# A transformer kernel whose first stage projects values in fp32 and keys as three products of rounded and remaining parts

## The reference, cut to what matters

```
x = x + matmul(fake_quant(layernorm(x)), fake_quant(ctx))            # layer 0 "attention", per batch
x = x + mx_linear(silu(mx_linear(n, w_gate)) * mx_linear(n, w_up), w_down)     # n = layernorm(x)
    # mx_linear quantises its input to 6 bits and its weight to 4 bits, with one exponent per 32 values
k = ctx @ wk    # 8 key heads of 128, 2 batches of 512 context rows
v = ctx @ wv    # 8 value heads of 128
x = x + softmax(rope(q) rope(k)^T / sqrt(128)) v @ wo                # 32 query heads
x = x + (silu(n @ gate) * (n @ up)) @ down                           # layer 1, ternary weights
```

## Time and profile before

| | us |
|---|---|
| median of three runs | 702.56 (700.72 to 702.59) |
| the profiled execution | 702.53 |
| its span, first to last instruction | 700.7 |
| PE busy | 668.3 (95%) |
| DVE busy | 520.0 (74%) |
| POOL busy | 463.3 (66%) |
| ACT busy | 363.3 (52%) |

### The profile page before, as it was taken

The page is one execution under the profiler, slowest core; times in us unless marked ns, Lnnn a source line. Parts: engine busy times, 40 slices in busy tenths (PEclk is TensorE's granted clock), DMA queues, the critical chain, the costliest instruction groups (busy, mean ns, idle before and its releaser), DMA issues.

```text
span 700.7 us, 11095 instructions
## 1 busy us (share of the span) xinstructions
PE 668.3 (95%) x3152; PEld 494.0 (70%) x3152; DVE 520.0 (74%) x1046; ACT 363.3 (52%) x686; POOL 463.3 (66%) x407
## 2 busy tenths in 40 slices
PE   6999998899899999999999999999999999799997
PEld 2444443444577788888888888888888877688885
DVE  4999798777668888888888888888888886721122
ACT  2697434533565665666666665665665663211110
POOL 0697426432479878778789788688698478066661
PEclk9999999999999999999999999999999999999999
DMA  9985422140323132141131221221223012013311
GB/s 340 343 293 183 134 87 80 36 155 6 127 71 119 30 106 76 30 134 45 55 110 45 82 83 45 90 75 46 89 75 135 17 31 66 25 46 101 113 56 61
DMA packets 39420, 67.27 MB, mean 96 GB/s; under 512 B 3680, under 2 KB 12000, under 8 KB 38368
## 3 DMA queue, kind: packets, MB, share of 16 engines
q1 hardware_dynamic: 39392, 66.93, 28.9%
HBM read 57.48 MB, written 9.44 MB: 95 GB/s over the span
## 4 chain that ended last, share of the span: by engine, by line
PE 71%; POOL 10%; DVE 8%; issue 7%; ACT 2%; DMA 1%; SPq 0%; POOLq 0%; DVEq 0%; ACTq 0%
PE ps L663 16%; PE ps L665 16%; PE ps L664 16%; PE ps L731 11%; PE ps L696 7%; POOL mx_raw L1104 3%; POOL mx_w L1110 3%; PE ps L584 2%; PE ps L520 1%; DMA X<-in_x 1%; PE ps L536 1%; POOL prob L1161 1%; PE ps L620 1%; DVE mx_amax L1339 1%; DVE stats L1260 1%
## 5 line engine op out<-in xcount | busy, mean ns | idle before, releaser
L1009 ACT ACTIVATE prob<-ps,nmax 128x512 f32<-128x512 f32 x128 | 88.3, 690 | 97.4 <-DVE nmax L1487 97.0
L1161 POOL TENSOR_SCALAR prob<-prob,rinv 128x512 f32<-128x512 f32 x128 | 89.4, 698 | 73.7 <-DVE rinv L1494 73.6
L731 PE MATMUL ps<-xt,wq_sb 128*128 128x512 f32 x384 | 103.2, 393 | 3.8 <-DVE q_cos L1502 2.1
L1020 ACT CAST pT<-ps 128x512 fp32r<-128x512 f32 x128 | 75.1, 587 | 52.8 <-PE ps L696 51.9
L1487 DVE CUSTOM_DVE_ANT_0 ps<-ps,mask_sb 128x512 f32<-128x512 f32 x128 | 87.9, 687 | 6.7 <-PE ps L665 6.3
L1508 DVE TENSOR_TENSOR pT<-ps,pT 128x512 fp32r<-128x512 f32 x128 | 86.3, 674 | 3.0 <-ACT pT L1020 2.0
L731 PEld LDWEIGHTS ps<-xt,wq_sb 128*128 128x128 f32 x384 | 71.6, 188 | 22.0 <-issue 4.6
L696 PE MATMUL ps<-idf,prob 128*128 128x128 f32 x512 | 76.7, 272 | 0.4 <-POOL prob L1161 0.3
L696 PEld LDWEIGHTS ps<-idf,prob 128*128 128x128 f32 x512 | 63.8, 141 | 17.3 <-POOL prob L1161 1.6
L520 PE MATMUL ps<-ctxT,wk_sb 128*128 128x512 f32 x128 | 60.5, 613 | 6.5 <-DMA ctxT<-in_ctx_cols 6.5
L1104 POOL TENSOR_TENSOR mx_raw<-mx_raw,mx_r 128x2048 f32<-128x2048 f32 (+1 forms) x9 | 30.2, 3354 | 53.7 <-DVE mx_r L1347 53.7
(11 more groups left out here) (177 smaller groups left out, 1587.9 us busy)
## 6 DMA issues: line engine op xcount, KB each, us to landing
mx_raw<-in_mxw SPq DMA_DIRECT2D x8, 1024.0 KB, 5.5
wq_raw<-in_wq SPq DMA_DIRECT2D x32, 256.0 KB, 3.2
wo_raw<-in_wo SPq DMA_DIRECT2D x32, 256.0 KB, 2.7
v_scr<-v_st SPq DMA_DIRECT2D x16, 256.0 KB, 2.5
kr<-k_scr SPq DMA_DIRECT2D x16, 256.0 KB, 2.9
vr<-v_scr SPq DMA_DIRECT2D x16, 256.0 KB, 3.4
k_scr<-k_st SPq DMA_DIRECT2D x14, 256.0 KB, 2.1
kr_swp<-k_scr SPq DMA_DIRECT2D x28, 128.0 KB, 3.3
```

Source lines behind the costliest of these rows:

```text
L731: last = mm(query_bank(H), wq_sb[:, par, l, k], xt[:, r, k], start=(n == 0), stop=(n == 11))
L1009: nc.scalar.activation(prob[:, j], bank(j % 2), ACT.Exp, bias=nmax[:, j:j + 1], scale=-1.0, accum_out=rsum[:, j:j + 1]).then_inc(exps, 1)
L1020: copy(pT[:, v % 2, 0, :, i * P:(i + 1) * P], bank(2 + i % 2).rearrange("p (k c) -> p k c", k=4)).then_inc(ph_ready, 1)
L1161: nc.gpsimd.tensor_scalar(prob[:, i], prob[:, i], rinv[:, i:i + 1], 1.0, ALU.mult, ALU.mult).then_inc(probs, 1)
```

## The change

- `STEPS` is new: all sixteen value units come first, in fp32 as before (half 0 of all eight context tiles, then half 1), then eleven key units. The first four value units are computed together, slice by slice (`first_values`).
- SP loads `x` first, then the context and the value weights of batch 0 in four slices of 128 rows each, with the scalars and the first weight chunk between them.
- Keys are three fp32r products of high and low parts: `high*high + high*low + low*high`, twelve MATMULs a unit. The high part is a rounded copy, made on ACT (`context_high`, two passes of 1024 columns for each batch; `weights_high`, 512 columns for each of eight heads). The low part is the difference, on POOL (`context_low`, `weights_low`).
- The parts lie in the memory of what is dead by then: `ctx_lo` over the context itself, `ctx_hi` over the value weights.
- The second of the two exponent operations (`mx_r`) moves from DVE to POOL (`exponents`, ahead of each `scale_in`).
- Key head 0 is computed in loops 5 and 6, and `key_rotate` moves to the ends of POOL's loops 5 and 6. The tiles of layer 1's attention are laid out anew.

```diff
+STEPS = (
+    ([("v", 0, 0), ("v", 1, 0), ("v", 2, 0), ("v", 3, 0)], [("v", 4, 0)]),
...
+    ([("v", 7, 1), ("k", 1, 0)], [("k", 2, 0)]),
+    ([("k", 1, 1), ("k", 2, 1)], [("k", 0, 0)]),
+    ([("k", 0, 1), ("k", 3, 0)], [("k", 3, 1)]),
+    ([("k", 4, 0), ("k", 4, 1), ("k", 5, 0)], []),
+)
...
+V_LAST = 4
+
+HIGH_AT = {V_LAST - 1: (0, 1), V_LAST: (2, 3), V_LAST + 1: (4, 5), V_LAST + 2: (6,)}
...
             def key_part(i, b, n, parts):
+                pe.wait_ge(wk_split, HEADS.index(i) + 1)
+                _, high, low = wk_parts(i)
+                cols = slice(b * CTX, (b + 1) * CTX)
                 for k in parts:
-                    last = mm(bank(n), wk_sb[:, i % 2, k], ctxT[:, k, b * CTX:(b + 1) * CTX], start=(k == 0), stop=(k == KD - 1))
+                    if i == HEADS[0] and k % 2 == 0:
+                        pe.wait_ge(ctx_split, 2 * b + k // 2 + 1)
+                    last = three(bank(n), [high[:, k], low[:, k]], [ctx_hi[:, k, cols], ctx_lo[:, k, cols]], k == 0, k == KD - 1)
...
             for i in range(1, NFULL):
                 copy_unit(STEPS[i][0][0])
+                if i == V_LAST:
+                    context_high(1)
                 mx_lift(i + 1, 0)
...
+                if i == V_LAST - 2:
+                    context_high(0)
+                for turn in HIGH_AT.get(i, ()):
+                    weights_high(HEADS[turn])
+            weights_high(HEADS[7])
             keep_quantised(1)
...
+            def exponents(i):
+                n, p = width(i) // BLK, i % NRAW
+                pool.wait_ge(mx_expo, i + 1)
+                ts(mx_r[:, p, 0:n].bitcast(I32), mx_e[:, p, 0:n].bitcast(I32), -1.0, -(2.0 ** 24), ALU.mult, ALU.add).then_inc(mx_scale, 1)
...
+            def context_low(b):
+
+                if b == 0:
+                    pool.wait_ge(v_sums, VALUES.index((3, 1)) + 1)
+                cols = slice(b * CTX, (b + 1) * CTX)
+                for k in range(0, KD, 2):
+                    pool.wait_ge(ctx_high, 2 * b + k // 2 + 1)
+                    tt(ctx_lo[:, k:k + 2, cols], ctxT[:, k:k + 2, cols], ctx_hi[:, k:k + 2, cols].bitcast(F32), ALU.subtract).then_inc(ctx_split, 1)
+
+            def weights_low(i):
+                raw, high, low = wk_parts(i)
+                pool.wait_ge(wk_high, HEADS.index(i) + 1)
+                tt(low, raw, high.bitcast(F32), ALU.subtract).then_inc(wk_split, 1)
...
             scale_in(0)
             scale_in(1)
-            key_rotate(0)
-
             for i in range(NFULL):
                 if i + 2 <= NFULL:
                     scale_in(i + 2)
                 if i == L0_AT + 2:
                     fp6_out(q1[:].rearrange("p t d -> p (t d)"), NT * D, 0, q1_ready)
                 scale_out(i)
-                if i == 0:
-                    key_rotate(1)
+                if i == V_LAST - 2:
+                    context_low(0)
+                for turn in HIGH_AT.get(i, ()):
+                    weights_low(HEADS[turn])
+                if i == V_LAST - 1:
+                    context_low(1)
+                if i in (V_LAST + 1, V_LAST + 2):
+                    key_rotate(i - V_LAST - 1)
+            weights_low(HEADS[7])
             scale_out(NFULL)
```

More of the change, by code:

```diff
@@ L52 @@
 VALUES = [unit[1:] for step in STEPS for part in step for unit in part if unit[0] == "v"]
-KEYS_AT = {1: 2, 2: 3, 4: 4, 5: 5}
+KEYS = [unit[1:] for step in STEPS for part in step for unit in part if unit[0] == "k"] + list(LATE_KEYS)
+STORED_KEYS = [key for key in KEYS if key[0] > 0]
+HEADS = [head for head, batch in KEYS if batch == 0]
 Q_AT, L0_AT = 1, 4
+V_LAST = 4
+HIGH_AT = {V_LAST - 1: (0, 1), V_LAST: (2, 3), V_LAST + 1: (4, 5), V_LAST + 2: (6,)}
 EXP_MASK = 0x7F800000
@@ L175, in build @@
                 int_T = sb("int_T", [P, 2, IPAD], BF16, b)
+                wk_hi01 = sb("wk_hi01", [P, 2, KD, DH], F32R, b)
+        with ExitStack() as a:
+            ctx_lo = sb("ctx_lo", [P, KD, CTOK], F32R, a)
+            wk_lo01 = sb("wk_lo01", [P, 2, KD, DH], F32R, a)
+            sb("skip_k", [P, NSLOT * CTX], F32, a)
+            ctx_hi = sb("ctx_hi", [P, KD, CTOK], F32R, a)
+            with ExitStack() as b:
+                wk_23 = sb("wk_23", [P, 2, KD, DH], F32, b)
+            wk_lo23 = sb("wk_lo23", [P, 2, KD, DH], F32R, a)
+            wk_hi23 = sb("wk_hi23", [P, 2, KD, DH], F32R, a)
         with ExitStack() as a:
@@ L287, in rotating @@
         def rotating(unit):
+            if unit == ("v", 0, 0):
+                return 0
             return ROTATE[place[unit] % len(ROTATE)]
@@ L435, in _ @@
             values_load(0, 1)
-            k_load(7)
             wq_load(2, 0)
@@ L659, in turn_rows @@
                             last.then_inc(xh_turned, 1)
-            def three(out_ap, left, right, first, final):
-                mm(out_ap, left[0], right[0], start=first, stop=False)
-                mm(out_ap, left[0], right[1], start=False, stop=False)
-                return mm(out_ap, left[1], right[0], start=False, stop=final)
             turn_rows()
@@ L856, in swap @@
             def swap(b):
-                act.wait_ge(k_sums, b + 1)
+                act.wait_ge(*keys_summed(0, b))
                 n = key_bank(0, b)
@@ L912, in copy_unit @@
                 kind, i, j = unit
-                if kind == "k":
+                if kind == "k" and i == 0:
+                    swap(j)
+                elif kind == "k":
                     copy_keys(i, j)
@@ L916, in copy_unit, with context_high, weights_high @@
                     copy_values(i, j)
-            swap(0)
+            def context_high(b):
+                act.wait_ge(v_sums, NCT * (b + 1))
+                cols = slice(b * CTX, (b + 1) * CTX)
+                for k in range(0, KD, 2):
+                    copy(ctx_hi[:, k:k + 2, cols], ctxT[:, k:k + 2, cols]).then_inc(ctx_high, 1)
+            def weights_high(i):
+                raw, high, _ = wk_parts(i)
+                turn = HEADS.index(i)
+                act.wait_ge(wk_in[turn % 4], 16 * (turn // 4 + 1))
+                copy(high, raw).then_inc(wk_high, 1)
+            rows_scale()
+            mx_lift(0, 0)
+            mx_lift(0, 1)
             copy_values(0, 0)
             copy_values(1, 0)
-            mx_lift(0, 0)
-            mx_lift(0, 1)
-            rows_scale()
-            copy_values(2, 0)
             act.wait_ge(id_in, 16)
```

161 lines of the change are left out of this document (96 added, 65 removed), and 11 rows, old and new, of the table STEPS.

## The result

The kernel after the change takes 707.17 us (median of 4 runs, 706.2 to 708.08), the kernel before 702.58 (4 runs): a ratio of 1.0071, 95% interval 1.0047 to 1.0095. The forecast was 709.7. The direction was right, the size was 2.5 us too large.

A forecast was written before the change was run, and what follows sets the result against it. Before 190 us two chains arrive almost together, PE's units and DVE with POOL; the second decides, DVE waiting beside POOL. 5.2 + 3.7 - 1.7 = +7.2 us on 702.5 gives 709.7, range 698.5 to 713.5.

The forecast's parts named there:

- Start: Loading: x no longer stands behind 1.31 MB, DVE starts at 5.6 instead of 9.52; -4.0 us for all engines at loop 3.
- Key units: PE's keys: twelve fp32r products take 2.85 us where a unit cost 3.43; 0.6 us less for each of 16 units.
- Loops 3 to 5: DVE's waits beside POOL use up the 4.0 us lead, then cost 7.0 with 5.8 back: +1.25 us at scale_in(7).
- Loop 6: In fp6, DVE's small operations wait for one POOL operation each; fp6_out comes later, gate_up starts at 127.0: +5.2 us.
- Loop 7 and the feed-forward: fp6 of row tile 0 waits for scale_out(7), the last weights_low and scale_out(8); slice (1, 2) moves +3.7 us more.
- Late keys: Cheaper key units before gate_up(3), before the last rows' transpose and at 187.80: together -1.7 us.
- A: Rival: the port shared by DVE and POOL costs nothing, the -4.0 us lead holds through loop 5; 697.8 us, chance 0.22.
- B: Rival: DVE waits in loops 6 and 7 only, the 4 us lead is left at scale_in(7); 704.5 us, chance 0.16.
- C: Rival: context_low costs 3.64 us instead of 2.35, or POOL keeps the port pair through a run; 714.9 us, chance 0.10.

The follow-up runs named there:

- no_low: Kernel after without POOL's twelve subtractions (context_low, weights_low), PE taking the rounded parts again in their place; 699.72 us, ratio 0.9958 to the kernel before.
- small_psum: Kernel after with the small fp6 operations of the feed-forward's first row tile on PSUM operands instead of SBUF; 705.21 us, ratio 1.004 to the kernel before.
- fp32_keys: Kernel after with keys as fp32 products of the raw parts again, without the splitting on ACT and POOL; 701.69 us, ratio 1.0004 to the kernel before.
- best: fp32_keys with key_rotate split up and moved into the feed-forward, one key unit ahead of PE's wait for chunk 5; 702.33 us, ratio 0.9995 to before.
- best_late: best_adds_last with one more key unit moved from the first stage into the feed-forward; 701.69 us, ratio 0.9992 to the kernel before.
- best_adds_last: best with its two sums of head 0's keys moved from behind fp6_out of row tile 2 to tile 3; 704.48 us, ratio 1.0024 to before.

## Why the prediction was right, and where its size was off

- **Start.** DVE started at 6.29, not 5.6, and chunk 3's rounding at 51.56, not 50.75: a lead of 3.2 us instead of 4.0. Waits in loops 3 to 5 that were shorter than forecast made up for these 0.8 us, so the close match at `scale_in(7)` is in part luck.
- **Key units.** 2.76 to 2.8 us at full clock (forecast 2.75 to 2.85). What I left out is that PE, made to wait, then runs at a lower clock (0.62 and 0.70 in 85 to 95, 0.66 in 110 to 115), and is slow once more in `gate_up` (0.71 in 125 to 130). This is why PE was ready for `fp6_out` at 122.8 and not at 121. It cost the sum nothing, because POOL was later each time; that was not foreseen either.
- **Loops 3 to 5.** Forecast waits of 4.65 us (both clips of loop 3) and 7.0, so 11.65; measured 10.97 by the comparison with no_low (4.31 and 6.66). Given back by waits for ACT and PE that went: 6.2 (forecast 5.8). L1440 at 91.31 (91.55), `scale_in(7)` at 101.63 (101.75), chunk 5 on PE at 108.94 (109.05). One detail was wrong: the context's clip L1413 slipped in at 58.54 unhindered, the clip of the chunk and the exponents paid for it.
- **Loop 6.** The first small operation passed in 0.20 us at the end of `scale_out(5)`, the next three and L1480 stood for one POOL operation each. `fp6_out` started 11.6 us after the first small operation (forecast 11.9), `gate_up` at 126.78 (127.0): +4.99 for the forecast +5.2.
- **Loop 7 and the feed-forward.** The step that failed in size: slice (1, 2) came at +7.77 instead of +8.9, so this term is +2.8 instead of +3.7. The three waits came, for `scale_out(7)`, `weights_low` and `scale_out(8)`, but POOL was through its list earlier: `scale_out(7)` ended at 136.86, not 137.7, the third wait at 139.13, and product (1, 0) was read at 141.95, not 143.1. DVE reached these waits at 136.19, later than the forecast 134.7, behind a `gate_up` at low clock; so they held it for 2.3 us and not for 5.35, and its lateness vanished in them.
- **Late keys.** From +7.77 to +5.89: -1.9, forecast -1.7. The 0.3 for half a unit before `gate_up(3)` is in it as forecast (+7.47 there, 156.85 against 149.38).
- **Not in the sum: the end.** From DVE's last operation to the end of the span it takes 4.2 us in the profiled execution of before and 2.5 us in that of after. This gives back 1.7 us that no part of the change was meant to touch. The forecast had no term for it, and it brought the measured time further below the forecast.
- **Not in the sum: the clock later.** In the profiled execution the granted clock fell to 0.84 and 0.82 in 605 to 615, which cost 1.4 us (+5.68 before it, +7.11 at DVE's last operation). Whether it does so in the executions without a profile is not known.

5.0 + 2.8 - 1.9 = +5.9 in the middle (measured +5.68), less 1.7 at the end, plus 0 to 1.4: +4.0 to +5.4, and the medians say +4.6. The stated range, 698.5 to 713.5, also held no change at all, so falling inside it shows little; the starts in the trace are the better test of the account.

Of the rivals, A took all of POOL's added work to be free and put `gate_up` at 118.9; without the subtractions, but with the rotates, no_low has it at 121.49. What stands between A and the kernel after is DVE's waiting beside POOL. B had the whole lead left at `scale_in(7)`; it came 1.1 us later than before, behind DVE's stretched operations in loops 3 to 5. C is refuted in both forms: two `context_low` took 5.19 us together, including a wait, where it had 7.3, and DVE's operations slipped in one by one instead of standing through POOL's run. (The prediction's price for this second form, 5.2 us, does not fit the 1 us that it gives it for loop 6.)

## What to carry to other kernels

An engine's idle time is not free room if its work shares a path with the engine that sets the time. Before moving work to POOL, look at what DVE does beside it: in these traces reductions and operations on PSUM operands passed, and a chain of small SBUF operations paid one POOL operation per step. To put such POOL work beside DVE's long reductions is what follows from this, but no run tested it alone. Putting the chain's small operands into PSUM gave 1.7 us in small_psum.

When two chains arrive almost together, shortening one brings the time of the other, and a wait moved onto PE may lower its clock besides.

## What the runs showed of the hardware that I had not expected

- A DVE operation on 4 columns of SBUF takes 0.16 us alone and 1.17 to 1.22 us beside back-to-back POOL operations of 1.27 us; small operations on 44 columns of PSUM take 0.21 us beside a POOL operation of 3.64 us (small_psum). POOL waits in turn: L1206 took 3.16 us instead of 1.27.
- PE's granted clock goes to its lower level after an idle of 3.27 us (0.62 in 85 to 90) and of 4.09 us (0.66 in 110 to 115). With the second idle filled by 17 products it stays at 1.00 there. In `gate_up`, behind idles of only 1.34 and 1.57 us, it is low again (0.71 in 125 to 130, 1.7 us more for the first products); the cause of this one is open.
- The end of the span comes either 2.5 to 2.6 us or 4.1 to 4.6 us after DVE's last result. DVE's last rows, of before and of after, whose spans end at 700.7 and 706.1:

```profile
693.68 2.79 DVE L1578 SCALAR_TENSOR_TENSOR res<-ps,sc,X 128x512 f32<-128x512 f32 x4 [1.22 <-PE ps L665]
```

```profile
700.78 2.80 DVE L1677 SCALAR_TENSOR_TENSOR res<-ps,sc,X 128x512 f32<-128x512 f32 x4 [1.22 <-PE ps L568]
```

  Among the 14 profiled executions the longer end is found in four (before, fp32_keys, best, best_late). In these four the DMA view has a packet of the instruction queue between DVE's last result and the end of the span, in before at 696.8 to 697.0. In best_adds_last this packet comes about 1 us after the end of the span (699.2 against 698.3), and the end is short; the other nine have neither. Whether the fetch causes the longer end is not settled, but the two go together in all 14.
